# Counting edges in half windows: 25 destinations with five chunks each, in place of 50 with eight

## The reference

```
h   = relu(layernorm(x))                       # 1250 x 512
# layer 0: edge mean, linear attention over the first 256 rows, batch norms
xn  = batchnorm(h)
agg = segment_sum(xn[src], dst) / max(deg, 1)
conv = relu(agg @ W_conv + b_conv)
q, k, v = h_dense @ Wq, @ Wk, @ Wv             # 8 heads of 64
qf, kf = exp(u - diag - max(u)) / 16 + 1e-6    # u = q or k times proj; max per row, or over a head
attn = (qf @ (kf.T @ v)) / (qf @ sum(kf)) @ Wo
x   = x + batchnorm(conv + attn + h)
# layer 1: edge sum, two matmuls with batch norms
h   = relu(layernorm(x)); agg = segment_sum(h[src], dst); h = (1 + eps) * h + agg
x   = x + relu(batchnorm(relu(batchnorm(h @ W1 + b1)) @ W2 + b2))
```

## Time and profile before

| | |
|---|---|
| median of 3 runs | 403.9 us (403.88 to 404.29) |
| profiled execution | 404.43 us, span 402.6 us |
| TensorE busy | 379.6 us (94%) |
| VectorE busy | 233.1 us (58%) |
| ScalarE, GpSimd busy | 172.7 us, 95.3 us |
| code one-hots (L859) | 200, 54.0 us |
| lane comparisons (L854) | 25, 18.7 us |
| count matmuls | 200, 46.7 us |
| granted TensorE clock | full in all slices |

### The profile page before, as it was taken

One profiled execution on the slowest core, in us unless ns is written; L12 is line 12 of the kernel. 1 busy time (PEld: TensorE's weight loads), 2 busy tenths in 40 slices (PEclk: granted clock), 3 DMA queues, 4 the chain that ended last, 5 costly groups with the idle time before them and its releaser, 6 DMA issues.

```text
span 402.6 us, 5977 instructions
## 1 busy us (share of the span) xinstructions
PE 379.6 (94%) x1987; PEld 279.1 (69%) x1987; DVE 233.1 (58%) x615; ACT 172.7 (43%) x301; POOL 95.3 (24%) x149
## 2 busy tenths in 40 slices
PE   2799999998999999999998998899999999999995
PEld 1587555664655565676755665456999999999992
DVE  5887598745464588672797888711344535421324
ACT  1446536757466413512006577511445453333031
POOL 7130011000000000000003488952165654201100
PEclk9999999999999999999999999999999999999999
DMA  6960200000000000000390002300000003010222
GB/s 189 290 202 25 106 2 2 2 1 2 1 0 3 2 2 1 2 2 2 96 243 24 2 8 99 107 2 1 0 2 0 2 0 106 0 50 16 64 53 76
DMA packets 16577, 17.96 MB, mean 45 GB/s; under 512 B 1813, under 2 KB 10965, under 8 KB 16537
## 3 DMA queue, kind: packets, MB, share of 16 engines
q1 hardware_dynamic: 15779, 17.28, 15.3%
q10 hardware_dynamic: 758, 0.16, 0.2%
HBM read 14.88 MB, written 2.56 MB: 43 GB/s over the span
## 4 chain that ended last, share of the span: by engine, by line
PE 75%; DVE 10%; issue 6%; ACT 3%; POOL 3%; DVEq 1%; DMA 0%; SPq 0%; POOLq 0%; ACTq 0%
PE bank L1201 73%; DVE ring L859 1%; DVE hl L1089 1%; POOL ln_s L435 1%; DVE w_lo L1108 1%; POOL x L473 1%; PE bank L1222 1%; DVE st L939 1%; DVE st_row L1100 1%; PE bank L1553 1%; DVE x L1097 1%; ACT hh L713 1%; DVE st_row L819 1%; PE bank L1382 1%; DVE x L1171 1%
## 5 line engine op out<-in xcount | busy, mean ns | idle before, releaser
L1201 PE MATMUL bank<-AT,hh 125*128 125x400 f16 (+1 forms) x240 | 80.9, 339 | 2.6 <-DVE hl L1089 2.6
L1201 PE MATMUL bank<-AT,hl 125*128 125x400 f16 (+1 forms) x240 | 80.7, 338 | 0.0
L444 POOL TENSOR_TENSOR bn_tmp<-var_eps,minus_half 128x1 f32<-128x1 f32 (+1 forms) x15 | 9.6, 642 | 202.6 <-DVE var_eps L945 202.5
L859 DVE TENSOR_SCALAR ring<-iota_code,code 125x500 f16<-125x500 f16 x200 | 54.0, 345 | 0.0
L1201 PE MATMUL bank<-ring,S 125*128 125x500 f16 x200 | 46.7, 376 | 0.0
L854 DVE TENSOR_TENSOR S<-iota_lane,slo 125x1024 f16<-125x1024 f16 x25 | 18.7, 748 | 43.1 <-PE bank L1201 36.4
L1201 PEld LDWEIGHTS bank<-ring,S 125*128 125x128 f16 x200 | 28.5, 144 | 18.3 <-issue 6.5
L1201 PEld LDWEIGHTS bank<-AT,hh 125*128 125x128 f16 x240 | 23.2, 97 | 21.7 <-DVE hl L1089 3.2
L1201 PE MATMUL bank<-wC,hn 128*125 128x512 f32 x80 | 36.0, 592 | 0.0
L1201 PEld LDWEIGHTS bank<-AT,hl 125*128 125x128 f16 x240 | 23.3, 97 | 18.1 <-issue 0.2
L1201 PE MATMUL bank<-a_hi,w_hi 128*128 128x400 f32 (+1 forms) x96 | 34.2, 356 | 0.0
(11 more groups left out here) (196 smaller groups left out, 692.8 us busy)
## 6 DMA issues: line engine op xcount, KB each, us to landing
x_in<-x SPq DMA_DIRECT2D x5, 448.0 KB
x<-x SPq DMA_DIRECT2D x2, 1120.0 KB
w_s<-w SPq DMA_DIRECT2D x2, 1024.0 KB, 9.6
w_s<-w SPq DMA_DIRECT2D x4, 512.0 KB, 3.8
out<-x SPq DMA_DIRECT2D x8, 224.0 KB
wB<-wk SPq DMA_DIRECT2D x1, 1024.0 KB, 8.2
wA<-wq SPq DMA_DIRECT2D x1, 1024.0 KB, 12.3
wC<-w_conv SPq DMA_DIRECT2D x1, 1024.0 KB, 15.2
```

The source lines that it names most:

```text
L444: own.step(pool.tensor_tensor(bn_tmp[:, 1, k:k + n], var_eps[:, k:k + n], minus_half[:, 0:n], ALU.pow))
L859: ins = dve.tensor_scalar(ring[:, slot, j, :], iota_code[0:CH], code[:, bass.ds(c + j, 1)], float(-CODES * t), ALU.subtract, ALU.is_equal)
L1201: return pe.matmul(o, l, r, start=start, stop=stop, skip_group_check=True)
```

## The change

A window's 50 destinations become two halves of `HW = 25`, each with its own range of chunks and `G = 5` chunks. Codes of a half are 250. For each window and half VectorE copies five chunks of `code` (now lane and code as a pair, both f32) to a fixed place `cw`, waits for the copies once, and then makes five lane one-hots of 125 x 128, one for each chunk and side by side, and five code one-hots of 125 x 250, with scalars at fixed addresses; `s_hot` is raised after each half. TensorE does ten matmuls of 250 columns, each half into its own 250 columns of the bank. Ranges are worked out for 50 halves, with a third column of chunks over five, and each window takes two register loads of three numbers on VectorE and on TensorE. Copies to `AT` and the low counts go over `h`, the halves. The diff, cut:

```diff
-G = 8
-Q = 4
+G = 5
 W = 50
-CODES = T * W
+HW = W // 2
+NH = 2 * NW
+CODES = T * HW
...
-        iota_lane = place("iota_lane", [P, P, G], F16, 1.25)
+        iota_lane = place("iota_lane", [P, P], F16, 1.25)
-        ranges = place("ranges", [NW, 2], I32, 6.6875)
+        ranges = place("ranges", [NH, 3], I32, 6.6875)
-        ring = place("ring", [CH, 2, G, CODES], F16, 112.75)
-        S = place("S", [CH, 2, P, G], F16, 128.5)
+        ring = place("ring", [CH, 2, 2 * G, CODES], F16, 112.75)
+        S = place("S", [CH, 2, 2 * G, P], F16, 128.5)
-        code = place("code", [CH, NCH + G], F32, 205.75)
-        slo = place("slo", [CH, NCH + G], F16, 206.4375)
+        code = place("code", [CH, NCH + 2 * G, 2], F32, 126.875)
+        cw = place("cw", [CH, 2, 2, G, 2], F32, 126.625)
...
+        def counts_of(t):
+            return banks[COUNT_BANK[t]][0:L, 0:2 * CODES].rearrange("p (h a b) -> p h a b", h=2, a=T)
+
+        def at_of(A, t):
+            return A[:, :, t * W:(t + 1) * W].rearrange("p a (h b) -> p h a b", h=2)
...
             own.step(dve.scalar_tensor_tensor(rng_f[:, 2:3], rng_f[:, 1:2], 1.0, red[:, 1:2], ALU.add, ALU.max))
+            own.step(dve.tensor_tensor(rng_f[:, 3:4], rng_f[:, 2:3], rng_f[:, 1:2], ALU.subtract))
+            own.step(dve.tensor_scalar(ranges[:, 2:3], rng_f[:, 3:4], float(-G), 0.0, ALU.add, ALU.max))
             dve.sem_inc(sem("s_ranges"), 1)
-            dve.tensor_tensor(rng_f[:, 3:4], rng_f[:, 2:3], rng_f[:, 1:2], ALU.subtract).then_inc(sem("s_span"), 1)
-
-            def lanes(slot, c):
-
-                a = slo[:, bass.ds(c, G)].unsqueeze(1).broadcast_to([CH, P, G])
-                dve.tensor_tensor(S[:, slot], iota_lane[0:CH], a, ALU.is_equal)
-
-            def one_hots(slot, t, c, done):
+
+            def code_of(slot, half, c):
+                return dve.tensor_copy(cw[:, slot, half], code[:, bass.ds(c, G), :])
+
+            def one_hots(slot, t, half, to):
 
                 for j in range(G):
-                    ins = dve.tensor_scalar(ring[:, slot, j, :], iota_code[0:CH], code[:, bass.ds(c + j, 1)],
-                                            float(-CODES * t), ALU.subtract, ALU.is_equal)
-                    if j % Q == Q - 1:
-                        ins.then_inc(done, 1)
+                    dve.tensor_scalar(S[:, slot, to + j, :], iota_lane[0:CH], cw[:, slot, half, j, 1:2], None, ALU.is_equal)
+                for j in range(G):
+                    ins = dve.tensor_scalar(ring[:, slot, to + j, :], iota_code[0:CH, 0:CODES], cw[:, slot, half, j, 0:1],
+                                            float(-CODES * (2 * t + half)), ALU.subtract, ALU.is_equal)
+                return ins
...
             def load_range(t):
-                dve.load([lo_r[t % 2], hi_r[t % 2]], ranges[t:t + 1, :])
+                for h in range(2):
+                    dve.load([lo_r[t % 2][h], hi_r[t % 2][h], more_r[t % 2][h]], ranges[2 * t + h:2 * t + h + 1, :])
 
             def first_chunks(t):
 
-                lo = dve.snap(lo_r[t % 2], min_val=0, max_val=NCH - 1)
                 if t >= 2:
                     dve.wait_ge(sem("s_win"), t - 1)
-                lanes(t % 2, lo)
-                one_hots(t % 2, t, lo, sem("s_hot"))
+                for h in range(2):
+                    own.mark(code_of(t % 2, h, dve.snap(lo_r[t % 2][h], min_val=0, max_val=NCH - 1)))
+                own.after(own.n)
+                for h in range(2):
+                    one_hots(t % 2, t, h, h * G).then_inc(sem("s_hot"), 1)
                 dve.reg_add(made, made, 1)
...
                 further_chunks(t)
-                dve.reg_sub(span_r, hi_r[t % 2], lo_r[t % 2])
...
-            def count(ps, t, j, start, stop):
-                return mm(ps[:, 0:CODES], S[:, t % 2, :, j], ring[:, t % 2, j, :], start, stop)
+            def count(ps, t, h, j, start, stop):
+                return mm(ps[:, h * CODES:(h + 1) * CODES], S[:, t % 2, j, :], ring[:, t % 2, j, :], start, stop)
...
-                pe.load([lo_r, hi_r], ranges[t:t + 1, :])
-                pe.reg_add(rest_r, lo_r, G)
+                for h in range(2):
+                    pe.load([lo_r[h], hi_r[h], more_r[h]], ranges[2 * t + h:2 * t + h + 1, :])
+                pe.reg_add(span_r, more_r[0], more_r[1])
                 ps = banks[COUNT_BANK[t]]
-                for j in range(G - 1):
-                    if j % Q == 0:
-                        pe.wait_ge(sem("s_hot"), G // Q * t + j // Q + 1)
-                    count(ps, t, j, j == 0, False)
+                for j in range(2 * G - 1):
+                    if j % G == 0:
+                        pe.wait_ge(sem("s_hot"), 2 * t + j // G + 1)
+                    count(ps, t, j // G, j, j == 0, False)
```

More of the change, by code:

```diff
@@ L42 @@
 Y_OF = [next(j for j, (a, b) in enumerate(Y_TILES) if a <= i < b) for i in range(T)]
-WIN_SHIFT, WIN_MUL = 16, 1311
+WIN_SHIFT, WIN_MUL = 17, 5243
 TILE_SHIFT, TILE_MUL = 17, 1049
-assert all(d * WIN_MUL >> WIN_SHIFT == d // W and d * TILE_MUL >> TILE_SHIFT == d // L for d in range(N))
-assert NCH == 160 and L * T == N and W * NW == N and CODES <= 512 and BIG * CH <= 2048
+assert all(d * WIN_MUL >> WIN_SHIFT == d // HW and d * TILE_MUL >> TILE_SHIFT == d // L for d in range(N))
+assert NCH == 160 and L * T == N and W * NW == N and 2 * CODES <= 512 and BIG * CH <= 2048
 PARAMS = [("n1g", FB), ("n1b", FB), ("n2g", FB), ("n2b", FB), ("bc", FB),
@@ L688, in _ @@
                     act.wait_ge(sem("s_win"), t + 1)
[L689 to L690 removed]
+                    copy(at_of(AT, t), counts_of(t)).then_inc(sem("s_at"), 1)
             for f in range(FB):
@@ L805, in _ @@
             own.step(dve.tensor_scalar(quo[:, 1], quo[:, 1], TILE_SHIFT, None, ALU.logical_shift_right))
-            own.mark(dve.scalar_tensor_tensor(code_r[:, 0], quo[:, 0], float(CODES - W), edge[:, 0], ALU.mult, ALU.add))
+            own.mark(dve.scalar_tensor_tensor(code_r[:, 0], quo[:, 0], float(CODES - HW), edge[:, 0], ALU.mult, ALU.add))
             own.mark(dve.scalar_tensor_tensor(code_r[:, 2], quo[:, 1], float(-L), edge[:, 1], ALU.mult, ALU.add))
@@ L828, in _ @@
             ps = read_group(dve, "codes")
-            own.mark(dve.tensor_copy(code[:, 0:NCH], ps[0:CH, 0:NCH]))
-            n_slo = dve.tensor_copy(slo[:, 0:NCH], ps[0:CH, NCH:2 * NCH])
-            free_group(n_slo, "codes")
+            free_group(dve.tensor_copy(code[:, 0:NCH, :].rearrange("p c a -> p a c"),
+                                       ps[0:CH, 0:2 * NCH].rearrange("p (a c) -> p a c", a=2)), "codes")
             ps = read_group(dve, "ranges")
-            own.step(dve.tensor_scalar(sel[:, 0, :], ps[0:NW, 0:NCH], win_of_lane[:, 0:1], None, ALU.is_le))
-            ins = dve.scalar_tensor_tensor(sel[:, 1, :], ps[0:NW, NCH:2 * NCH], win_of_lane[:, 0:1],
+            own.step(dve.tensor_scalar(sel[:, 0, :], ps[0:NH, 0:NCH], win_of_lane[:, 0:1], None, ALU.is_le))
+            ins = dve.scalar_tensor_tensor(sel[:, 1, :], ps[0:NH, NCH:2 * NCH], win_of_lane[:, 0:1],
                                            sel[:, 0, :], ALU.is_ge, ALU.mult)
@@ L870, in attention @@
                     ps = read_group(dve, name)
-                    own.mark(dve.tensor_reduce(most[:], ps[0:1, 32:32 + NW], AX.X, ALU.max))
+                    own.mark(dve.tensor_reduce(most[:], ps[0:1, 32:32 + NH], AX.X, ALU.max))
                     free_group(dve.tensor_copy(diag[:], ps[:, 0:32].rearrange("p (a n h) -> p a h n", a=2, n=2)), name)
@@ L948, in _ @@
             made = dve.alloc_register("groups_made")
[L949 to L951 removed]
+            copied = dve.alloc_register("codes_copied")
+            dve.reg_mov(copied, 0)
+            lo_r = [[dve.alloc_register(f"first_chunk{k}{h}") for h in range(2)] for k in range(2)]
+            hi_r = [[dve.alloc_register(f"last_chunk{k}{h}") for h in range(2)] for k in range(2)]
+            more_r = [[dve.alloc_register(f"chunks_over{k}{h}") for h in range(2)] for k in range(2)]
+            span_r, big_r = dve.alloc_register("chunks_over"), dve.alloc_register("exact_chunks_over")
+            none_r = dve.alloc_register("none_over")
             rest_r = dve.alloc_register("further_chunks")
[L953 removed]
+            dve.reg_mov(big_r, BIG - G)
+            dve.reg_mov(none_r, 0)
             dve.reg_mov(made, 0)
@@ L1432, in _ @@
             seen = pe.alloc_register("seen")
-            lo_r, hi_r = pe.alloc_register("first_chunk_pe"), pe.alloc_register("last_chunk_pe")
+            lo_r, hi_r, more_r = ([pe.alloc_register(f"{what}_pe{h}") for h in range(2)]
+                                  for what in ("first_chunk", "last_chunk", "chunks_over"))
+            span_r, none_r = pe.alloc_register("chunks_over_pe"), pe.alloc_register("none_over_pe")
+            pe.reg_mov(none_r, 0)
             most_r, big_r = pe.alloc_register("most_chunks"), pe.alloc_register("exact_chunks_pe")
@@ L1469, in _ @@
                     pe.sem_inc(sem("s_grp"), 1)
```

(2 more changed lines are left out.)

83 lines of the change are left out of this document (41 added, 42 removed).

## The result

The changed kernel took **418.4 us** (median of 4 runs, 416.11 to 419.05), the kernel before 403.9 (4 runs, 403.87 to 404.29): ratio 1.035, 95% interval 1.031 to 1.039. I had forecast 407.3 and a range of 400 to 414. The direction was right; the size was off by 11 us and outside the range. The profiled execution took 416.11 us (span 414.3), 11.7 more than that of the kernel before; the other three have a mean granted clock of 0.973 instead of its 0.981, and take 1.8 to 2.9 us more. An execution over 1.5% slower than its kernel's fastest counts as slow and is left out of medians; two in experiment 5 are.

A forecast was written before the change was run, and what follows sets the result against it. VectorE's single queue, with maxima and `hh` behind the one-hots, was taken to bound the counting stage. 5.9 + 0.1 - 2.6 = +3.4 us on the profiled 404.43 gave 407.8, 407.3 as median; own range 404.7 to 412, wider 400 to 414.

The forecast's parts named there:

- The price: VectorE's one-hots: lanes 0.163, codes 0.195 us each; 3.75 us a window against 2.76, so 1.0 us more.
- TensorE's count: Ten matmuls of 250 columns, 0.107 us apart with 97 ns loads: 1.07 us, a gain of 0.63 a window.
- The coupling through the maxima and `hh`: In VectorE's queue, maxima stand behind next-window one-hots; ScalarE's `hh` waits for them, TensorE's R for `hh`; stood 2.1 us before.
- One of my signs of being wrong: Listed signs: lane plus code one-hot at 0.33 us or less, `hh` not behind the maxima, or TensorE waiting for `s_hot`.
- Setup: Ahead of window 0: two dependent steps (0.35 us) and one more register load (0.53), 0.9 us; GpSimd's memsets and iotas 0.
- R1 is late by 5.9 us: VectorE's lag makes UQ1's last maximum 8.0 us late; 2.2 us between `hh` and R1 leaves R1 5.9 late.
- The walk: Tally of VectorE's lag by window: 12.3 us through window 10, less waits of 0.25, 0.9 and 3.1, then 2.2 before R1.
- From 83 to 137 us: +0.1: Waits for `hh` before R3, R6 and R8 add 2.6 us; savings of windows 10, 12, 13, 15 take 2.5.
- From 137 to 186 us: -2.6: Eight windows could save 5.1 us; VectorE's loop of 5.9 us and the count bank's release lose half.
- B: Rival: VectorE's codes run at 0.52 ns an element, 0.65 us more a window, 417.7 us; chance 0.10.
- C: Rival: TensorE's weight loads stay at 144 ns, so its gain is missing; +3 us, 410.3 us; chance 0.08.
- A: Rival: VectorE's short comparisons are cheap, 394.5 us; chances 0.12 for 392 to 399, 0.18 for 399 to 403.1.

The follow-up runs named there:

- experiment 5: The changed kernel without the copies to a fixed place, its one-hots reading scalars at register addresses: 425.3 us, median of two executions.
- experiments 2: The kernel before with each code one-hot of 500 columns made in two of 250, all else kept: 411.6 us, ratio 1.019.
- experiment 3: The changed kernel with the slot's maxima ahead of the next window's one-hots in four VectorE loops: 403.91 us; kernel before with that order: 401.05 us.
- experiment 1: The changed kernel with GpSimd's low-count memset delayed past VectorE's first operation: 413.47 us; kernel before with that memset moved early: 406.23 us.
- experiment 6: The kernel before with every register load of a range written twice on VectorE and TensorE, though the second loads were not in what ran: 403.32 us.
- experiment 7: The changed kernel with 30 extra matmuls of 256 columns in TensorE's wait before V1: 415.45 us.
- experiment 4: The changed kernel with one lane comparison for each half, codes at register addresses and no copies: 400.26 us, ratio 0.991.

## Why the prediction was half right

**What held.** The price: lanes 0.163 and codes 0.195 us, exactly as forecast, 3.86 us (window 4) and 3.92 (window 5) against 3.75; in window 5 0.07 of the rest is the copies with their wait (0.34, not 0.27). TensorE's count: 1.09 against 1.07, loads 97 ns. No second rounds. The coupling through the maxima and `hh`, shown by experiments 2 and 3, and the waits before R1 (2.9, forecast 3), R3, R6 and R8. VectorE busy up by 31.5, forecast 25. One of my signs of being wrong did come: TensorE waited for `s_hot`, before the second halves of windows 5 and 7, 2.0 us in all.

**What failed, term by term** (profiled executions, +11.7 us against +3.4). The coupling was right; what was wrong is the price of the start (2.4 us too low), TensorE's clock (3.1 us, put at nothing) and the release of the count bank with the two loads behind it (1.9 us too low):

- *Setup, "0.9 us" and "GpSimd's memsets and iotas shrink, ahead of need: 0".* The first one-hot work started at 19.17 instead of 15.86: 3.3 late. 1.5 is the collision (experiment 1, 19.17 to 17.71): GpSimd's faster iota moved the memset onto VectorE's first operation. The gap ahead of window 0 is 2.35 against 0.98, 1.4 more, where I had 0.53 for the second load; both loads have a third number, and take 0.99 and 0.76 us.
- *"R1 is late by 5.9 us".* Measured 8.7. The walk itself stands: with 3.3 at the start and 1.1 a window it gives 3.3 + 12.1 + 0.4 - 4.25 - 2.2 = 9.3. 2.4 of the 2.8 missed is the start, the rest the 0.1 a window.
- *"From 83 to 137 us: +0.1".* From R1 (+8.7) to window 17's count (+11.3) it is 2.6. The waits before R3, R6 and R8 were 2.5, 1.2 and 2.5 us instead of 1.0, 0 and 1.0, 4.1 more. That is near the walk, which had 2.6 and let them swallow three counts' savings besides, 4.5 together. What it put at nothing is TensorE's clock, which falls behind the waits before R1 and R8 (granted 0.82 from 92 to 100 us, 0.86 from 137 to 149; in experiment 3, without these waits, 1.00). From R1 to window 10's count it takes 1.5 us longer than before, from R8 to window 17's 1.7: 3.1 us of clock. 4.1 + 3.1 less eight counts' savings of 0.61 is 2.4 of the 2.6.
- *"From 137 to 186 us: -2.6".* Measured -0.7 (11.3 to 10.6): seven savings are 4.3, and windows 20 and 22 took 3.6 back. TensorE stood 1.56 and 1.71 us before them, for its own two loads of 0.78 us each (experiment 6). In the setup I had set the second to 0 because its sequencer runs ahead, and in this walk both to 1.3; behind a released bank they lie bare. And the walk had VectorE's `s_lo` release the bank, where it was ScalarE's copy, behind exponentials that wait for VectorE's maxima: the coupling of `hh` once more.
- *After 186 us, "nothing".* 1.1 us more, within what executions of the kernel before differ by (spans 401.0 to 402.7).

Together 8.7 + 2.6 - 0.7 + 1.1 = 11.7. The median of the runs lies 2.3 above the profiled one, with the lower clock.

**V1** I had not walked at all, only R1: `vaug` stood behind UQ0's exponentials as `hh` behind UQ1's. Its wait and slow matmuls are inside R1's lag and add nothing (experiment 7: R1 at 92.05 with them and without).

**The rivals.** B's price (codes at 0.52 ns an element) did not come, though its 417.7 us lies near the result: the right number by the wrong cause. C is refuted by experiment 4 in its mechanism too (and its "every 16-bit load" near 97 ns overlooks those of `neg_id`, 135 ns in the kernel before). A's short operations are not cheap; but its side was reachable, by 0.77 us less a window and little of the collision (400.3).

## What to carry to other kernels

When an engine with slack is given more work, look at what stands *behind* that work in its queue and not at its total idle time: here 1.04 us a window cost 7.9 us under 36 us of waits, and moving four blocks gave the changed kernel 14.5 us, 12.6 more than it gave the kernel before. Halving a tile doubles the number of operations, registers and loads that have a fixed price (0.13 us an operation with a scalar, 0.23 us a register here); one broadcast comparison for five chunks (0.61 us) beat five lone ones (0.82), and needed no copies. When an edit makes an engine *faster*, check what its next instruction now falls beside.

## What the runs showed of the hardware

- A memset of 2.71 us on GpSimd held up an int32 `tensor_scalar` of VectorE until it ended (2.69 us instead of 0.29 to 0.35). With two iotas behind the memset the operation was held for 3.34 us, until the last of the three had ended.
- A register load takes VectorE 0.54 us for two numbers and 0.76 for three, TensorE 0.55 and 0.78.
- 16-bit weight loads of 138 and of 97 ns give the same 0.109 us between matmuls of 250 columns.
- After three stands of TensorE in 7.2 us, 5.8 in all, the granted clock was 0.68 from 58 to 66 us (so part of it ran at the lower level of 1.2 GHz); with the last stand filled it stayed at 1.00 (2.4 GHz).
- One-hots at an address from a register start as densely as at fixed places, but the sequencer spends a step on each (medians 46 and 83 ns); the register loads behind them were then no longer hidden.
